# Stacking transfers of a weight moved into the attention stage, and text stores shared by two DMA queues

## The reference

```
h = concat(patches(x) @ W + b, layernorm(word[ids] + pos + tables))      # 64 x 93 x 192
h = h + attention(layernorm(h))        # w = x @ w_qkv; per head: norms over tokens, softmax over tokens,
                                       # out = -(w * Pi) / (1 + sum(Pi * w*w)); out @ w_out + b_out
h = h + ffn(layernorm(h))              # 8 groups x 64 units: z = x @ P, scores, top 4, W1 (16 x 32 per unit),
                                       # gelu, W2, weighted by softmax; gelu(comb @ G1) @ G2
```

## Time and profile before

| | us |
|---|---|
| median of 3 runs | 1391.74 |
| lowest, highest | 1387.41, 1393.82 |
| profiled execution, its own time | 1385.12 |
| span of the profiled execution | 1383.4 |
| mean granted clock of PE in it | 0.956 of full speed |
| PE busy, share of span | 1228.8, 89% |
| DVE busy | 1101.5, 80% |
| ACT busy | 1086.2, 79% |
| POOL busy | 998.8, 72% |

### The profile page before, as it was taken

One profiled execution on the slowest core, in us unless ns is written; L12 is line 12 of the kernel. 1 busy time (PEld: TensorE's weight loads), 2 busy tenths in 40 slices (PEclk: granted clock), 3 DMA queues, 4 the chain that ended last, 5 costly groups with the idle time before them and its releaser, 6 DMA issues.

```text
span 1383.4 us, 34221 instructions
## 1 busy us (share of the span) xinstructions
PE 1228.8 (89%) x12232; PEld 625.2 (45%) x12232; DVE 1101.5 (80%) x3370; ACT 1086.2 (79%) x2696; POOL 998.8 (72%) x713
## 2 busy tenths in 40 slices
PE   2943799999999999868999999999999999999996
PEld 2942566666666666523343333333343333333332
DVE  5682488888888888957888888888888888888884
ACT  0243467777777667549999999999999999999994
POOL 7741367656775676637888888788888888888884
PEclk7975899999999999969999999999999999999998
DMA  9663312222322222143313322232413223232410
GB/s 274 161 133 74 60 49 84 67 67 74 99 65 68 73 94 67 51 114 88 71 44 86 68 59 65 57 76 53 97 46 90 64 58 65 57 81 51 95 39 12
DMA packets 95705, 107.06 MB, mean 77 GB/s; under 512 B 12772, under 2 KB 92668, under 8 KB 95254
## 3 DMA queue, kind: packets, MB, share of 16 engines
q1 hardware_dynamic: 86576, 94.95, 26.3%
q10 hardware_dynamic: 6848, 6.13, 2.6%
q0 software_dynamic: 2112, 3.79, 1.1%
HBM read 67.88 MB, written 33.71 MB: 73 GB/s over the span
## 4 chain that ended last, share of the span: by engine, by line
PE 21%; ACT 19%; DVE 13%; issue 3%; POOL 1%; SPq 1%; DMA 0%; POOLq 0%; DVEq 0%
ACT ring L1025 12%; DVE arena L1488 11%; PE ring L1741 9%; PE code L1775 9%; ACT arena L1037 6%; PE ring L1794 2%; PE ring L1785 1%; DVE arena L1496 0%; PE code L1662 0%; DMA gate_scales<-arena 0%; ACT arena L1033 0%; POOL arena L764 0%; SPq L611 0%; DVE arena L1273 0%; POOL arena L772 0%
## 5 line engine op out<-in xcount | busy, mean ns | idle before, releaser
L1488 DVE TENSOR_TENSOR arena<-ring,arena 128x496 f32<-128x496 f32 x1008 | 611.8, 668 | 123.4 <-ACT ring L1025 118.7
L827 POOL TENSOR_TENSOR arena<-arena 128x992 f32<-128x992 f32 x264 | 611.5, 2329 | 121.4 <-ACT arena L1037 111.5
L1025 ACT ACTIVATE ring<-ring 128x496 f32<-128x496 f32 x1008 | 544.5, 686 | 18.6 <-PE ring L1741 18.6
L1741 PE MATMUL ring<-arena,w_stack 99*32 99x496 bf16 x6144 | 424.9, 376 | 24.9 <-DVE arena L1488 18.0
L1775 PE MATMUL code<-arena,w_pad 128*32 128x496 f32 x3072 | 389.5, 580 | 8.3 <-DVE arena L1496 8.0
L1741 PEld LDWEIGHTS ring<-arena,w_stack 99*32 99x32 bf16 x6144 | 163.5, 95 | 400.9 <-DVE arena L1488 220.0
L1037 ACT ACTIVATE arena<-ring 128x992 f32<-128x992 f32 x252 | 283.4, 1125 | 0.8 <-PE ring L1741 0.7
L1592 PE MATMUL ring<-arena 96*128 96x372 f32 x384 | 136.3, 493 | 1.8 <-ACT arena L939 0.9
L1775 PEld LDWEIGHTS code<-arena,w_pad 128*32 128x32 f32 x3072 | 97.5, 110 | 59.7 <-DVE arena L1488 22.5
L764 POOL TENSOR_TENSOR arena<-arena 128x372 f32<-128x372 f32 x96 | 91.7, 986 | 32.9 <-DVE arena L1330 32.7
L1592 PEld LDWEIGHTS ring<-arena 96*128 96x128 f32 x384 | 72.1, 195 | 62.9 <-ACT arena L947 15.7
(11 more groups left out here) (143 smaller groups left out, 1418.1 us busy)
## 6 DMA issues: line engine op xcount, KB each, us to landing
arena<-gates SPq DMA_DIRECT2D x48, 496.0 KB, 6.6
gates<-arena SPq DMA_DIRECT2D x16, 744.0 KB, 11.5
arena<-h_scratch SPq DMA_DIRECT2D x32, 279.0 KB
arena<-z_parts SPq DMA_DIRECT2D x144, 62.0 KB, 2.6
h_scratch<-arena SPq DMA_DIRECT2D x16, 279.0 KB
z_parts<-arena SPq DMA_DIRECT2D x48, 93.0 KB, 2.1
arena<-h_scratch SPq DMA_DIRECT2D x12, 372.0 KB
out_h<-arena SPq DMA_DIRECT2D x12, 372.0 KB
```

The source lines that it names most:

```text
L827: p_.tensor_tensor(spaces[quad % SPACES][:, j:j + 2], hid[:, POOL_DUOS.index(duo) % 2], gst[:, block // EB, j:j + 2], ALU.mult).then_inc(s ...
L1025: a_.activation(product, product, ACT.Gelu_apprx_tanh).then_inc(s_hid, 1)
L1488: v_.tensor_tensor(spaces[quad % SPACES][:, j + p], duo_bank(duo, p), gst[:, block // EB, j + p], ALU.mult).then_inc(s_gat, 1)
L1741: mm = t_.matmul(bank[32 * q:32 * q + 32], w1s[:, x + 32 * q:x + 32 * q + 32], zst[:, o, j + p], start=True, stop=True)
```

## The change

`STACK_PARTS` gets three entries: part 0 behind chunk 5 of unit 0, parts 3 and 5 behind chunks 2 and 4 of unit 1. The loop of stage 1 no longer issues parts. The last of the four groups of W2 loads moves from step 8 to step 7, where it stands ahead of the cast of W1. For steps 7 to 10 SP issues two of the four text stores, and ACT the other two: those of step jj - 1 behind `mean_off(jj)`, those of step 10 behind ACT's whole loop. The semaphores count as before.

```diff
-STACK_PARTS = {(0, 3): 1, (0, 4): 4, (1, 3): 2}
+STACK_PARTS = {(0, 3): 1, (0, 4): 4, (0, 5): 0, (1, 2): 3, (1, 3): 2, (1, 4): 5}
 STACK_BIASES = {(1, 4): (0,), (1, 5): (1, 2)}
+SPLIT_FROM = 7
...
             def store_text(jj, par):
                 wait_apart(sp, (s_to, jj + 1))
-                for bb in range(4):
+                for bb in range(4 if jj < SPLIT_FROM else 2):
...
+            def store_text_rest(jj):
+                act.wait_ge(s_to, jj + 1)
+                for bb in range(2, 4):
+                    dst = h0_b[16 * bb:16 * bb + 16, NI + 7 * jj:NI + 7 * jj + 7, :]
+                    act.dma_start(dst, tout[:, jj % 2, bb]).then_inc(s_todma[jj % 2], 16)
+
             for jj in range(JJ):
                 mean_off(jj)
-                if jj in (4, 5, 6, 8):
-                    load_w2((4, 5, 6, 8).index(jj))
-                if jj >= 8:
-                    act.wait_ge(s_wc, 1)
-                    stack_part((0, 3, 5)[jj - 8])
+                if jj > SPLIT_FROM:
+                    store_text_rest(jj - 1)
+                if 4 <= jj < 8:
+                    load_w2(jj - 4)
...
+            store_text_rest(JJ - 1)
             stage1_over(act)
```

## The result

The changed kernel takes 1401.72 us (median of 8 runs, 1398.12 to 1405.01), the kernel before 1389.76 (8 runs, 1384.56 to 1393.82). The ratio is 1.0092, with a 95% interval of 1.0073 to 1.0112: 10 to 16 us slower (12.0 by the two medians), against 11.1 forecast.

A forecast was written before the change was run, and what follows sets the result against it. Bound: DVE's waits in the first 175 us, for ACT's cast, text stores and x0 loads. Hand-over 0.9, unit 0 4.2, unit 1 5.2 and clock 0.8 sum to 11.1 us on 1391.74: 1402.8 us, range 1393.5 to 1410 (8 in 10).

The forecast's parts named there:

- The cast of W1 is held by the issues: Step 7: eight W2 transfers issued ahead of ACT's cast make it, and DVE, 2.8 us late (bounds 0 to 4.2).
- The shared stores: Step 10: two stores a queue and no part in flight bring the first load 1.9 us sooner (bounds 0.5 to 2.6).
- The hand-over: From the text steps to the attention stage: late cast +2.8 and shared stores −1.9, together +0.9 us.
- Unit 0, +4.2: Third part ahead of x0 of unit 2 makes DVE start w_pi 4.17 us later (bounds 2.5 to 5).
- Unit 1, +5.2: Parts 3 and 5 joining part 2 make DVE start on x0 of unit 3 5.2 us late (bounds 3 to 7.05).
- The clock, +0.8: PE's granted clock falls after the longer stall in unit 1, half covered by DVE's work: +0.8 us (bounds 0 to 1.7).
- A load of SP that comes behind ACT's parts stands until these are through: Units 0 and 1: x0 waits for all queued parts, and DVE starts 4.8 us after their end.
- The prediction's estimate by turns: Units 0 and 1: engines alternating queues let 12 turns carry half of x0; the change costs 8.7 instead of 11.1 us.
- A: Rival: the stalls in the units are absorbed, only the hand-over or its gain stays; 1390 to 1392.7 us, 8%.
- C: Rival: queued parts hold ACT's own issues, 2 to 4 us in each unit; 1407 to 1411 us, 10%.
- B: Rival: x0 shares the engines with the parts, or the cast isn't held; 4 to 8 us, 1395.5 to 1399.5, 16%.

The follow-up runs named there:

- e2: The changed kernel with the last W2 loads back in step 8; 1400.00 us, ratio 1.0079 to the kernel before.
- e1: The changed kernel with stack parts 0, 3 and 5 back in steps 8 to 10; 1390.09 us, ratio 1.0016 to the kernel before.
- e10: The changed kernel with the three bias rows behind chunk 0 of unit 1, ahead of parts 3, 2 and 5; 1403.75 us, ratio 1.0111.
- e9: The changed kernel with 14 extra matmuls of no use on PE in the stall of unit 1; 1398.34 us, ratio 1.0085.
- e3: The changed kernel with part 0 issued after x0 of unit 2 instead of ahead of it; 1403.31 us, ratio 1.0103.
- e7: The changed kernel with each load of x0 and xr issued as two transfers, of 112 and 12 partitions; 1396.37 us, ratio 1.0070.
- e12: As e11, with parts 1 and 4 behind chunks 0 and 1 of unit 0 instead of 3 and 4; 1377.21 us, ratio 0.9923.
- e11: Changed kernel with the loads of e7, old unit parts, parts 0 and 3 and last W2 loads in step 8, part 5 in step 9; 1379.35 us.
- e5: The kernel before with parts 1, 4, 2 behind chunks 0 to 2 of unit 0, bias rows behind xT of unit 1; 1392.58 us, ratio 1.0039.
- e8: The kernel before with each load of x0 and xr issued as two transfers, of 112 and 12 partitions; 1381.05 us, ratio 0.9955.

## Why the prediction was right, and where it was not

*The cast of W1 is held by the issues: right.* +2.8 was forecast; the cast's idle time is 2.75 us, DVE's wait grew by 2.81, and e2, which takes the loads away, gives it back.

*The shared stores: right in the sum, its parts not shown.* A row was to land 3.15 us behind the shift, it took 3.13. The gain is 1.9 so measured, and 2.27 from the split of W1 on, as DVE's wait for PE ahead of step 10 (0.99 us) also went and a shorter one for ACT came (0.53). Of the 1.9 the forecast put 1.2 down to the halved issues and the rest to the part that no longer stands there. e1, which shares the stores and has the part back, gains 0.28 only: most of the gain hangs on the part's leaving. No run leaves all four stores to SP without a part in step 10, so what sharing is worth by itself stays open. The hand-over cost 0.55, forecast 0.9.

*Unit 0, +4.2: 3.6 in the marks, the mechanism right, the nearness in part luck.* DVE waited 9.94 us for x0 instead of 4.23, 5.7 more, but stood ready 2.1 us sooner. From the first part's issue to the statistics it is 19.40 us instead of 14.46: the third part cost 4.9, near the upper bound. 1.3 of that came back because the parts went out sooner in the unit; PE's granted clock was higher ahead of them (0.71 from 124.15 to 134.15 us; before, 0.53 from 123 to 133), for which the runs show no cause in the change.

*Unit 1, +5.2: mis-sized, 7.84.* This term was the furthest off. The shift of the queue's end was forecast well enough: 7.05, and 7.84 measured against the statistics of unit 2. But the forecast took the gap from the parts' end to DVE, 4.8 us, over from unit 0, though its own rows had 6.6 for unit 1 (166.5 to 173.13). By the last packets of data (166.22 before, 178.81 after) the gap is 6.91 us in both kernels, and in e1 and e2 too: in unit 1 the bias rows come last, and behind them q1 gets going slowly. With no other queue at work x0 moves 10 packets from 179 to 180 us, some 0.5 us each:

```profile
q1 hardware_dynamic: 10, 0.01, 32.5%
```

In unit 0, where a part comes last, the gap is 4.4 us before and 4.5 after, and in e10, with the rows in front, 4.7. So the gap did not shrink, as the forecast had it, but stayed. The upper bound, 7.05, took that and comes within 0.8 us.

*The clock, +0.8: half of the 1.72 measured.* It is the upper bound, 1.7: DVE's work covered none of it. e9, at full clock, has it back.

*The sum.* By the marks the change cost 13.8 us, by the medians 12.0, against 11.1; the misses in unit 1 and the clock make up the difference to the marks. That 1402.8 was forecast and 1401.72 measured is nearer than the terms are: it was reckoned from a median of 1391.74, and over 8 runs the kernel before has 1389.76.

*"A load of SP that comes behind ACT's parts stands until these are through": true for two and three parts, but not for the reason of order alone.* e3 put a part behind x0, and x0 was held all the same. On the Trainium skill's rule that each engine takes the queues in turn, a packet of each (DMA: Bandwidth & Descriptors, section Queues, rings and completion order), the runs are divided: in e3 both queues move packets in the same stretch, as it has it; from 134 to 147 us of the changed kernel they do not. Why an x0 that comes during two parts gets nothing, while a part that comes during x0 gets most, stays open; in e7, with x0 spread wider, it was still so (x0 issued at 137.26, its first packets after 145, with the parts' last). The prediction's estimate by turns also had a wrong count: 23 packets of x0 an engine are its 372 spread over 16, and on 4 engines it is 93, of which 12 turns would carry an eighth and not half.

Of the rivals A falls by the trace (no time after unit 4 came back) and C was not needed: ACT's issues behind parts lasted 0.55 to 0.59 us, those of the bias rows up to 1.14. It was SP that was held: the load of xr, behind x0 of unit 3, took 7.57 us to issue (at 176.81), where it took 0.66 before. B's mixing of queues does exist (e3), but as a cost.

## What to carry to other kernels

A transfer moved off a queue's busy place has to be costed against the loads of every other queue at its new place, not only against its own consumer: here the stack of W1 is not used before the third stage, over 400 us later, and the loss was in a load that has nothing to do with it. Read the share of a load that runs alone: 0.28 of the engines pointed to some four, and giving it all 16 by its shape was worth 5.3 us of the stretch in the kernel before, more than the one new order of the parts that helped (3.9, e12 against e11). And an instruction of an engine behind a row of DMA issues waits for all of them (2.75 us for the cast here), so issues belong behind the work that others wait for.

## What was not expected of the hardware

Three rows of 32 KB, each written into one partition, hold back another queue's load after their own packets are through: in the changed kernel 21 packets of x0 took some 0.5 us each from 179 to 181 us, with nothing else under way, against 0.04 us a packet later in the same load, and the gap behind the rows was 6.9 us against 4.4 to 4.7 behind a part. Why, no run shows; in e5, with parts and x0 among them, rows did not slow x0 so. And stage 1, whose program is the same in the kernel before, e5 and e8, reached the split of W1 at 86.70, 90.17 and 85.63 us: a scatter of that size is part of what the runs of one kernel differ by.
